# Normalising x rows and residual rows on GpSimd, and scaling the x part of the logits on ScalarE, in a cross-attention and mixture-of-experts kernel

## What is computed

```python
def reference(x, ctx_768, ...):
    x = x + _L0_xattn_ref(_layernorm(x, axis=-1), ctx_768, ...)
    x = x + _L0_ffn_ref(_layernorm(x, axis=-1), ...)
    return x

def _L0_xattn_ref(modality1, modality2, ln1_g, ln1_b, ln2_g, ln2_b, Wq, bq, Wk, bk, Wv, bv, Wo, bo):
    x1 = layernorm(modality1, ln1_g, ln1_b)
    x2 = layernorm(modality2, ln2_g, ln2_b)
    q = x1 @ Wq + bq
    k = x2 @ Wk + bk
    v = x2 @ Wv + bv
    scores = jnp.einsum('bqe,bke->bqk', q, k) * scaling
    attn = jax.nn.softmax(scores, axis=-1)
    return jnp.einsum('bqk,bke->bqe', attn, v) @ Wo + bo

def _L0_ffn_ref(x, ws1, bs1, ws2, bs2, We1, Be1, We2, Be2, Wr, br):
    shared = _gelu(x @ ws1 + bs1) @ ws2 + bs2
    aff = jax.nn.softmax(x @ Wr + br, axis=-1)
    vals, idx = jax.lax.top_k(aff, K)          # K = 3 of 31 experts
    ...                                        # sum over experts of gate * (gelu(x @ W1 + B1) @ W2 + B2)
    return shared + routed + x
```

## Time and profile before

| | us |
|---|---|
| median of 3 runs | 493.3 (491.27 to 494.15) |
| the profiled execution | 494.56 |
| its span in the trace | 492.9 |
| TensorE, VectorE busy | 461.0, 357.1 |
| GpSimd, ScalarE busy | 308.7, 253.7 |
| first stage, nine steps | 51.75 |

### The profile page before, as it was taken

How to read it: one execution, slowest core, us unless ns; L and a number is a source line. 1 busy time by engine, 2 the same in 40 slices (tenths; PEclk the granted TensorE clock), 3 DMA queues, 4 the chain that set the end, 5 groups by cost and what they waited for, 6 DMA issues and landing times.

```text
span 492.9 us, 13620 instructions
## 1 busy us (share of the span) xinstructions
PE 461.0 (94%) x3168; PEld 400.0 (81%) x3168; DVE 357.1 (72%) x1614; ACT 253.7 (51%) x848; POOL 308.7 (63%) x316
## 2 busy tenths in 40 slices
PE   8899979999999998879999999999999999999991
PEld 8677757777777877668999898899999999999891
DVE  4958879999999997773567666666666666661784
ACT  1455747676767667462445454445554555543220
POOL 3312385858585857671588888788888888884000
PEclk9999999999999999989999999999999999999997
DMA  7555668877578944893599999898888888875999
GB/s 241 150 172 151 219 208 255 274 239 257 189 235 286 334 149 154 276 360 105 116 184 187 185 183 181 157 145 138 136 137 137 139 135 138 136 107 101 350 348 322
DMA packets 81151, 97.54 MB, mean 198 GB/s; under 512 B 9201, under 2 KB 65906, under 8 KB 81074
## 3 DMA queue, kind: packets, MB, share of 16 engines
q1 hardware_dynamic: 60786, 70.79, 46.9%
q0 software_dynamic: 19248, 25.40, 30.8%
q10 hardware_dynamic: 1040, 0.48, 0.5%
HBM read 54.91 MB, written 41.73 MB: 196 GB/s over the span
## 4 chain that ended last, share of the span: by engine, by line
PE 50%; DVE 15%; issue 10%; DMA 10%; SPq 5%; POOL 3%; ACT 2%; POOLq 0%; DVEq 0%; ACTq 0%
PE bank L1271 12%; PE bank L1282 12%; DMA sum<-y_sb,token 6%; PE bank L1260 3%; PE bank L1106 2%; PE bank L1107 2%; PE bank L1118 2%; DVE w_all L792 2%; PE bank L1158 2%; DMA xt<-expert_rows_in 2%; POOL sum L579 2%; DVE c L741 2%; DMA w_all<-sum 2%; PE bank L1186 2%; PE bank L1159 2%
## 5 line engine op out<-in xcount | busy, mean ns | idle before, releaser
L579 POOL DMA_INDIRECT sum<-y_sb,token x105 | 170.8, 1626 | 48.0 <-issue 24.1
L689 ACT ACTIVATE up<-bank,b_all 128x128 f32<-128x128 f32 x260 | 81.4, 364 | 102.2 <-PE bank L1271 66.1
L1271 PE MATMUL bank<-xtt,w1b 128*128 128x128 f32 x840 | 111.4, 276 | 0.3 <-ACT xtt L715 0.3
L1282 PE MATMUL bank<-w_all,up 128*128 x420 | 108.8, 382 | 0.1
L1271 PEld LDWEIGHTS bank<-xtt,w1b 128*128 128x128 f32 x840 | 102.1, 192 | 0.8 <-ACT xtt L715 0.5
L984 DVE TENSOR_SCALAR y_sb<-bank,gate,inverse 128x256 f32<-128x256 f32 x105 | 57.1, 544 | 55.4 <-PE bank L1282 54.7
L557 POOL DMA_INDIRECT expert_rows_in<-xt,slot x75 | 74.4, 992 | 24.6 <-issue 24.0
L1282 PEld LDWEIGHTS bank<-w_all,up 128*128 128x128 f32 x420 | 71.7, 191 | 6.1 <-issue 0.2
L976 DVE COPY w1b<-w_all 128x512 f32 x105 | 47.7, 454 | 18.1 <-PE bank L1271 7.5
L715 ACT ACTIVATE xtt<-bank 128x256 f32<-128x256 f32 x105 | 40.2, 384 | 39.3 <-PE bank L1260 38.7
L534 POOL TENSOR_TENSOR rs<-mv,eps_cols 128x5 f32<-128x5 f32 (+1 forms) x32 | 8.0, 252 | 62.2 <-DVE mv L849 62.0
(11 more groups left out here) (199 smaller groups left out, 883.4 us busy)
## 6 DMA issues: line engine op xcount, KB each, us to landing
xt<-expert_rows_in SPq DMA_DIRECT2D x105, 132.0 KB, 2.6
w_all<-in_w SPq DMA_DIRECT2D x47, 256.0 KB
w_all<-in_ctx SPq DMA_DIRECT2D x32, 288.0 KB, 3.1
w_all<-sum SPq DMA_DIRECT2D x15, 384.0 KB, 7.3
sum<-pad_rows SPq DMA_DIRECT2D x1, 3328.0 KB, 12.0
w_all<-in_x SPq DMA_DIRECT2D x25, 128.0 KB, 3.1
sum<-y_sb SPq DMA_DIRECT2D x25, 128.0 KB
sum<-xt SPq DMA_DIRECT2D x25, 128.0 KB
```

Of the source, the lines that this page charges most:

```text
L579: pool.indirect_dma_start(sums[s], bass.IndirectOffsetOnAxis(ap=token[sx][:, 0:1], axis=0), y_sb[sx][:, :], None, compute_op=ALU.add).then ...
L689: ins = act.activation(up[s][:, m * P:m * P + P], up_ps[s][:, m * P:m * P + P], ACT.Gelu, bias=b1_all[:, e, m:m + 1].rearrange("p o n -> p ...
L1271: mm = pe.matmul(up_ps[s][:, m * P:m * P + P], w[:, c * INTER + m * P:c * INTER + m * P + P], xtt[s][:, c * P:c * P + P], start=(c == 0), ...
L1282: mm = pe.matmul(down_ps[s], up[s][:, m * P:m * P + P], w, start=(m == 0), stop=(m == 1))
```

## The change

GpSimd makes the normalised x rows and the normalised residual rows in its own step i, directly behind the power that gives their scale: x rows of `starts(i+2)` (one step number ahead of where VectorE made them) and residual rows of `ends(i-3)` (likewise). The two waits for free buffers move with them, VectorE's aggregates wait until GpSimd has read the old ones, and the expert numbers (L802) wait for the residual rows. ScalarE makes the x part of the logits as the first instruction of its step. VectorE keeps everything else in its order.

```diff
@@ GpSimd, step(i), behind the power
+                x = starts(i + 2)
+                if x is not None:
+                    pool.wait_ge(ctx_rstd, i + 3)
+                    if x >= 2:
+                        pool.wait_ge(x_transposed, x - 1)
+                    pool.tensor_scalar(z1[x % 2], x_sb[x % 8], mv[i % 2][:, 3, 0:1], rs[i % 2][:, 1, 3:4],
+                                       ALU.subtract, ALU.mult).then_inc(x_norm, 1)
+                t = ends(i - 3)
+                if t is not None:
+                    s4 = t % SLOTS
+                    rated_wait(pool, t)
+                    if t >= SLOTS:
+                        o = t - SLOTS
+                        pool.wait_ge(h_out[s4], (o // SLOTS + 1) * 16)
+                        pool.wait_ge(scattered[s4], (o // SLOTS + 1) * 16 * TOP)
+                        pool.wait_ge(h_transposed, o + 1)
+                    alone(pool)
+                    pool.tensor_scalar(h_sb[s4][:, 0:D1], resid[s4][:, :], mv[i % 2][:, 4, 0:1], rs[i % 2][:, 1, 4:5],
+                                       ALU.subtract, ALU.mult).then_inc(h_made, 1)
@@ ScalarE, head of step(i)
+                t = ends(i - 3)
+                if t is not None:
+                    act.wait_ge(attn_made, t + 1)
+                    act.wait_ge(x_dev_made, t + 1)
+                    if t >= 2:
+                        act.wait_ge(parts_read, t - 1)
+                    act.activation(x_part[t % 2][:, :], attn_ps[:, RB:RB + NE], ACT.Copy,
+                                   scale=x_dev[:, t % 8:t % 8 + 1]).then_inc(x_part_made, 1)
@@ VectorE, step(i)
                     dve.wait_ge(attn_made, mixed + 1)
+                    dve.wait_ge(x_part_made, mixed + 1)
                     dve.reciprocal(rinv[m2][:, :], attn_ps[:, D1:D1 + 1]).then_inc(rinv_made, 1)
-                    dve.wait_ge(x_dev_made, mixed + 1)
-                    dve.tensor_scalar(x_part[m2][:, :], attn_ps[:, RB:RB + NE], x_dev[:, mixed % 8:mixed % 8 + 1], None,
-                                      ALU.mult).then_inc(x_part_made, 1)
...
                     dve.wait_ge(resid_stat6, mixed + 1)
+                    if ended(i - 5) > 0:
+                        dve.wait_ge(h_made, ended(i - 5))
...
                 if routed is not None:
-                    if routed >= SLOTS:
-                        o = routed - SLOTS
-                        dve.wait_ge(h_out[r4], (o // SLOTS + 1) * 16)
-                        dve.wait_ge(scattered[r4], (o // SLOTS + 1) * 16 * TOP)
-                        dve.wait_ge(h_transposed, o + 1)
+                    dve.wait_ge(h_made, routed + 1)
                     dve.wait_ge(top_idx, routed + 1)
...
-                if met_x is not None:
-                    s = met % 2
-                    if met_x >= 2:
-                        dve.wait_ge(x_transposed, met_x - 1)
-                    dve.tensor_scalar(z1[met_x % 2], x_sb[met_x % 8], mv[s][:, 3, 0:1], rs[s][:, 1, 3:4],
-                                      ALU.subtract, ALU.mult).then_inc(x_norm, 1)
...
                     if new_x is not None:
+                        if new_x >= 2:
+                            dve.wait_ge(x_norm, new_x - 1)
                         dve.bn_aggr(mv[n2][:, 3, :], x6[new_x % 2][:, :])
...
-                if routed is not None:
-                    dve.tensor_scalar(h_sb[r4][:, 0:D1], resid[r4][:, :], mv[rp][:, 4, 0:1], rs[rp][:, 1, 4:5], ALU.subtract,
-                                      ALU.mult).then_inc(h_made, 1)
```

More of the change, by code:

```diff
@@ L735, in step @@
                 new, met, rated = batch(i + 2), batch(i + 1), batch(i - 1)
-                new_x, met_x = starts(i + 2), starts(i + 1)
+                new_x = starts(i + 2)
                 mixed, routed, ranked = ends(i - 3), ends(i - 4), ends(i - 5)
@@ L755, in step @@
                                              ALU.add).then_inc(resid_made, 1)
-                    dve.wait_ge(x_part_made, mixed + 1)
                     dve.scalar_tensor_tensor(logit_part[m2][:, :], attn_ps[:, RA:RA + NE], rinv[m2][:, 0:1], x_part[m2][:, :],
@@ L768, in step @@
                     rated_wait(dve, routed)
-                    rp = (i - 1) % 2
                     if routed >= 2:
                         dve.wait_ge(meta_made, routed - 1)
-                    dve.scalar_tensor_tensor(rec[r2][:, 0:NE], logit_part[r2][:, :], rs[rp][:, 1, 4:5], br_s[:, :], ALU.mult,
+                    dve.scalar_tensor_tensor(rec[r2][:, 0:NE], logit_part[r2][:, :], rs[(i - 1) % 2][:, 1, 4:5], br_s[:, :], ALU.mult,
                                              ALU.add).then_inc(logit_sum, 1)
```

## The result

| kernel | median us | lowest to highest | runs |
|---|---|---|---|
| before | 493.51 | 491.27 to 494.15 | 4 |
| after | 521.65 | 520.85 to 522.13 | 4 |

The ratio is 1.0577, with a 95% interval from 1.054 to 1.0614: slower by 5.8%. The profiled execution of the kernel after took 520.85 us and has a span of 518.8, against 494.56 and 492.9 before.

What follows compares the result with a forecast made beforehand. In the first stage TensorE and VectorE were taken as nearly full, relief bounded by TensorE's waits. Terms -3.3 + 2.2 + 1.0 + 0.5 = +0.4 gave 495.0 profiled, 493.7 as median; range 8 in 10: 489 to 503 us.

Steps and rivals of the forecast that it cites:

- GpSimd takes over as the bound: First stage, GpSimd's queue: at 0.9 us an operation 505 us; chance 0.27 together with the memory-port case.
- I take 0.57: GpSimd, each added 128x256 normalisation: 0.57 us, 14 in nine steps; from above some 0.9 us.
- Not all of the idle can be used: GpSimd, the two steps of nine without a scatter: 1.6 us stay idle, so 51.1 of 51.75 us are filled.
- It decides from 0.61 us: GpSimd's queue: the price an operation from which GpSimd would become the bound.
- About 1.5 us of slack: GpSimd's next power, awaited by VectorE's context rows: 1.5 us of slack, 1.0 more from VectorE's lost work, hides nearly all lateness.
- lateness in a run of scatters: GpSimd, successive scatter steps: some 2.3 us late after four, nearly all hidden; 0.3 us per nine steps, +1.0 us.
- The first scatter: GpSimd's queue there: two normalisations ahead of the power add 1.1 us, freed VectorE takes back half, so +0.5 us.
- VectorE's relief: First stage: VectorE loses three instructions a tile, TensorE's waits for x rows and L658 and the stage's end shrink, -3.3 us.
- ScalarE's head: Head of ScalarE's step: x part delays later copies 0.2 us in half of 22 tile steps, +2.2; rival 497 us, chance 0.09.
- Free: ScalarE's added wait for the attention product costs nothing, as TensorE issues that product before the transposes ScalarE waits for next.
- The port: GpSimd and VectorE at memory: each delays the other 0.3 us in five of seven tile steps, 497 us; chance 0.27 with GpSimd-bound case.
- if the new operations cost over 0.7: GpSimd's added normalisations: a price above 0.7 us each was named as showing the forecast wrong.

Runs made afterwards that it cites:

- idle work: Kernel before plus two tensor_scalar of 128x256 on GpSimd behind the power, results unread, nothing taken from VectorE: 519.67 us, ratio 1.0535.
- the run with 64 columns: Kernel before plus two unread tensor_scalar on GpSimd behind the power, 64 columns wide in place of 256: 497.78 us, ratio 1.008.
- the run for the relief: Changed kernel with GpSimd's two normalisations cut to 8 of 256 columns and the x part back on VectorE: 491.15 us, ratio 0.9956.

## Why the prediction was wrong

The forecast was 493.7 us, with 489 to 503 around it; the time is 521.65. The mechanism stood there as the rival "GpSimd takes over as the bound", with 505 us at its upper price. The steps:

**The price of the normalisation: the largest term that failed.** It was "I take 0.57", with an upper end of 0.9, both from a select of 128x128 in 0.286 us. It measured 1.29 to 1.30 us in the change and 1.23 as idle work: 2.3 times the value taken and 1.4 times the upper end. The row did not answer: the select is another operation, and doubling its width said nothing on two arithmetic operations with scalars read from columns. The price alone adds 14 x 0.73 = 10.2 us to nine steps. Its bounds were too narrow as well: twice the copy-like row for "two operations" is a guess about an engine, and a bound from rows as far as these should have gone on to where the case decides.

**"Not all of the idle can be used": 1.6 us, the second term that failed.** The forecast let VectorE need 2.2 us from the power to the next statistics, read in the earlier trace rows from a step without logits. In a step without a scatter in the middle of the stage it needs 3.5 us even before the change, from the logit sum L772 at 103.63 to the end of the statistics at 107.16, and 4.4 after it. So GpSimd waits 4.7 us in nine steps at 0.60 us an operation, and even at 1.30, where the forecast's own reasoning (2.9 us of work behind the power against 2.2) leaves no wait, 3.0. At the price taken nine steps would thus need some 41.5 + 8.0 + 4.7 = 54.2 us and not 51.1, an estimate from the run with 64 columns. "It decides from 0.61 us" failed with it: nine steps are 0.9 us longer already at 0.42. The measured 63.44 us are 41.5 + 18.1 + 3.0 = 62.6 and 0.8 that GpSimd stands idle ahead of L547.

**"About 1.5 us of slack": the wrong place.** It was read at the context rows L792, but VectorE's first instruction behind the power is the logit sum (L772 before), which starts 0.83 us ahead of them (101.48 to 102.31 in the kernel after). In the nine steps after, VectorE waits 7.3 us there and 0.8 at the context rows. The forecast's lateness in a run of scatters, +0.3 us in nine steps and +1.0 in all, went with it: with idle work at 0.60 us nine steps are 2.8 us longer.

**The first scatter, +0.5 us: the wrong sign.** In the six traces of kernels without an arithmetic tensor_scalar in GpSimd's steps, the first scatter starts behind a pause of 3.05 to 3.94 us; in the thirteen with one it is 0.18 or 0.19 us, whatever its width and whether or not its result is used. What the pause is, no run shows. It offsets part of what the steady steps lose, so that the whole time of the run with 64 columns (+4.0) and of the run for the relief (-2.2) look kinder to the forecast than their steady steps do.

**VectorE's relief, -3.3 us: the reason not borne out.** The run that comes nearest measured -2.2 us, and of TensorE's waits 2.0 us went as written, with the copy of q in the place of the x rows. But the waits for L658 grew (3.4 us in seven to 4.1 in eight) where the forecast had 0.7 less, the steady steps became longer, and the gain sits at the first scatter. That the number is near is luck. In the change itself nothing of the relief is left: TensorE waits 8.9 us for x rows out of GpSimd's queue. The 25 us less of busy time did not show either: 357.1 to 346.7 is 10.4 less. Instructions of VectorE overlap in the trace (three context instructions of 0.38 us stand there as 0.94 together), so 1.04 us of durations a tile is not 1.04 us of its time; the forecast did not rest on this.

**ScalarE's head, +2.2 us: not settled.** Alone it costs 3.9 us (between 2.6 and 5.1); with the relief it costs the difference of 1.0015 and 0.9956, 2.9 us, taken on two chips. The price on the queue (0.17 us) was right. "Free" for the added wait was not: ScalarE waits at it for the attention product, 4.4 us in five steps, and VectorE waits in turn for the x part ahead of its reciprocal, 2.0 us in the nine steps of the change. But the steady steps hardly grew by it (103.7 to 104.15 us in eighteen), so how it costs 3.9 us is not shown.

**The port: there, but not the main cause.** In this rival each of two engines holds up the other. The GpSimd operation took 1.23 us as idle work with VectorE fully loaded, 1.25 us behind the stage, 1.30 in the change. VectorE's context instruction in the nine steps, before and after:

```profile
L792 DVE TENSOR_SCALAR w_all<-w_all,mv,rs 128x192 f32<-128x192 f32 x28 | 9.2, 381 | 0.0
...
L817 DVE TENSOR_SCALAR w_all<-w_all,mv,rs 128x192 f32<-128x192 f32 x27 | 9.4, 405 | 1.0 <-POOL rs L536 0.8 <-issue 0.2
```

So 0.024 x 27 = 0.6 us of VectorE's nine steps and some 0.07 x 14 = 1.0 us of GpSimd's: less than 2 of 11.7 us. In the run with idle work of 256 columns it is more: the context instructions took 447 ns in nine steps, 1.8 us, and the casts of the expert numbers 278 ns against 158, 0.8 us, of 9.9 us in all. By the Trainium skill (SBUF — State Buffer, section Who interferes with whom) a VectorE instruction in a two-port mode and a GpSimd instruction exclude each other, and the later waits out the whole of the earlier. None of the context instructions is seen to have waited out 1.3 us: the longest of the 96 took 0.56 us in the kernel after, as in the kernel before.

**The Trainium skill's rule against the change** (GPSIMD Engine Reference, section Engine selection) had the right advice, elementwise work on VectorE, for a reason that does not cover this case: it calls one input roughly line rate. This case's traces do not agree. Against VectorE's 0.417 us, the same operation with one input took 1.30 us, three times as long, and an add of two inputs took 0.72, less than any of the four forms of one input with arithmetic.

What the text named as its own refutation, "if the new operations cost over 0.7", is what came. What stays open: the pause of the first scatter, why the residual rows alone (+10.6) cost 5 us more than the x rows alone (+5.5) with steady steps as long, and where ScalarE's head costs its 3.9 us.

## What to carry to other kernels

Before work is moved to an engine that is "only 60% busy", add up what one full step of it issues, gaps between the DMA issues included, and hold that against the step; then find the first instruction elsewhere that needs its result, and what stands behind that one. Idle time in the steps where the engine waits for its partner can't be lent to the steps where it is full: 10.2 us of waiting did not hold 5.9 us of work. Read such a wait in the very kind of step in which it counts. Where no row shows the operation on that engine, the price of another kind of operation is no bound: put the point from which the case tips inside the range, and give the side beyond it the chance that such ignorance deserves. And when a measured time agrees with a term, look in the trace whether it was won where the term said: here the length of nine steps said otherwise than the whole time.

## What was not expected of the hardware

- GpSimd's tensor_scalar with two operations and scalars from columns takes 1.23 to 1.32 us at 128x256 float32, 0.80 to 0.84 at 128 columns, 0.59 to 0.61 at 64 and 0.39 to 0.44 at 8: some 0.4 us and 3.3 ns a column.
- The form decides: 1.25 us with two operations and column scalars, 1.07 with constants, 0.92 and 0.84 with one operation, 0.72 for an add of two tensors, 0.39 for a copy.
- The pause of 3.05 to 3.94 us ahead of GpSimd's first indirect DMA is 0.18 to 0.19 us in every kernel whose steps have a tensor_scalar on GpSimd ahead of it, even one of 8 columns. The trace ascribes it to "issue"; its cause is not shown.
- TensorE's granted clock fell to 0.95 in the mean of the nine steps in which it paused 9.2 us, after 1.00 before; its busy time there rose from 48.90 us for 352 matmuls to 54.23 for 354. Most of the rise is not the clock: in the 62.7 us behind them, at 1.00, 349 matmuls were busy 51.67 us. Whether the clock cost anything can't be parted from the rest.
